# Loading phase and first step of an attention-and-experts kernel, rebuilt: weight halves, subtracts on GpSimd, a second token tile in a buffer of its own

## The reference

```
xn = layernorm(x)
q, k, v = xn@Wq, xn@Wk / sqrt(128), xn@Wv          # 8 heads, DK 128, DV 64
alpha   = sigmoid((xn@Wg + bg) / 16)               # one decay per token and head
state_t = alpha_t * state_(t-1) + k_t v_t^T ; o_t = q_t . state_t
attn    = (o * sigmoid(xn@Wog)) @ Wo
scores  = sigmoid(xn @ gate_w^T) ; sfc = scores + gate_bias
          # keep 4 of 8 groups by the sum of their two best sfc, then the 8 best of 64 experts
ffn     = sum over chosen e (at most 256 tokens each) of weight * (silu(xn@w_gate_e) * (xn@w_up_e)) @ w_down_e
out     = x + attn + ffn
```

## Time and profile before

| | |
|---|---|
| median of 3 runs | 1263.7 us |
| profiled execution, its own time | 1266.82 us |
| span of that execution | 1265.1 us |
| PE busy | 1237.9 us, 98% |
| PEld busy | 1092.2 us, 86% |
| DVE busy | 976.6 us, 77% |
| ACT busy | 624.3 us, 49% |
| POOL busy | 487.4 us, 39% |
| chain that ended last | PE 76%, DVE 16%, issue 5%, ACT 2% |
| DMA | 194.68 MB, mean 154 GB/s |

### The profile page before, as it was taken

One profiled execution on the slowest core, in us unless ns is written; L12 is line 12 of the kernel. 1 busy time (PEld: TensorE's weight loads), 2 busy tenths in 40 slices (PEclk: granted clock), 3 DMA queues, 4 the chain that ended last, 5 costly groups with the idle time before them and its releaser, 6 DMA issues.

```text
span 1265.1 us, 28662 instructions
## 1 busy us (share of the span) xinstructions
PE 1237.9 (98%) x9910; PEld 1092.2 (86%) x9910; DVE 976.6 (77%) x2343; ACT 624.3 (49%) x1319; POOL 487.4 (39%) x377
## 2 busy tenths in 40 slices
PE   7899999999999999999999999999999999999999
PEld 6788888887888888799899998989989999889987
DVE  6997878889797659878688687786885877868844
ACT  6675756666574544344444444444444444434432
POOL 2110111011001027237467385474574754845620
PEclk9999999999999999999999999999999999999999
DMA  6576534354352322357486575674774765748665
GB/s 241 170 250 200 188 110 156 122 190 158 121 171 60 111 75 84 95 145 186 105 198 165 130 178 136 150 181 106 188 171 121 172 155 137 193 104 191 162 194 183
DMA packets 124920, 194.68 MB, mean 154 GB/s; under 512 B 12016, under 2 KB 98608, under 8 KB 124592
## 3 DMA queue, kind: packets, MB, share of 16 engines
q1 hardware_dynamic: 94384, 147.99, 36.1%
q0 software_dynamic: 30464, 45.83, 19.7%
HBM read 148.62 MB, written 57.74 MB: 163 GB/s over the span
## 4 chain that ended last, share of the span: by engine, by line
PE 76%; DVE 16%; issue 5%; ACT 2%; another core or an unknown queue 0%; DVEq 0%; DMA 0%; ACTq 0%
PE bank L793 21%; PE bank L808 7%; PE bank L905 7%; PE bank L937 7%; PE bank L845 6%; PE bank L825 5%; PE bank L877 3%; PE bank L863 3%; PE bank L866 3%; PE bank L948 3%; PE bank L836 3%; DVE Dt L1506 3%; PE bank L889 2%; PE bank L927 2%; DVE At L1527 2%
## 5 line engine op out<-in xcount | busy, mean ns | idle before, releaser
L635 POOL DMA_INDIRECT acc<-arena,idx_all x128 | 224.3, 1752 | 149.4 <-DMA acc<-res 54.1
L627 POOL DMA_INDIRECT arena<-table,idx_all x132 | 163.6, 1240 | 153.8 <-ACT share L1160 96.5
L793 PE MATMUL bank<-xp,wq 128*128 128x512 f32 x768 | 208.4, 406 | 0.0
L793 PE MATMUL bank<-xp,wk 128*128 128x512 f32 x768 | 202.2, 398 | 0.0
L793 PEld LDWEIGHTS bank<-xp,wk 128*128 128x128 f32 x768 | 138.5, 188 | 29.3 <-DVE wk L1416 0.4
L793 PEld LDWEIGHTS bank<-xp,wq 128*128 128x128 f32 x768 | 136.6, 189 | 25.4 <-issue 0.8
L1506 DVE TENSOR_TENSOR_SCAN Dt<-decay,eye_b 128x512 f32<-128x512 f32 x128 | 157.7, 1233 | 0.0
L845 PE MATMUL bank<-qT,kT 128*128 128x128 f32 x1024 | 136.2, 275 | 1.8 <-DVE At L1527 1.4
L1136 ACT ACTIVATE kT<-bank 128x512 f32<-128x512 f32 x128 | 76.7, 599 | 118.0 <-PE bank L793 102.2
L845 PEld LDWEIGHTS bank<-qT,kT 128*128 128x128 f32 x1024 | 125.2, 192 | 3.3 <-DVE At L1527 1.6
L1136 ACT ACTIVATE qT<-bank 128x512 f32<-128x512 f32 x128 | 76.9, 601 | 85.4 <-PE bank L793 64.7
(11 more groups left out here) (174 smaller groups left out, 2317.1 us busy)
## 6 DMA issues: line engine op xcount, KB each, us to landing
decay<-decay_dram SPq DMA_DIRECT2D x64, 512.0 KB
carry<-decay_dram SPq DMA_DIRECT2D x60, 512.0 KB
arena<-in_L_attn_x_dram SPq DMA_DIRECT2D x16, 512.0 KB, 4.5
table<-arena SPq DMA_DIRECT2D x16, 512.0 KB, 3.2
xT_dram<-arena SPq DMA_DIRECT2D x16, 512.0 KB, 3.0
arena<-in_L_ffn_w_gate_dram SPq DMA_DIRECT2D x64, 128.0 KB
arena<-in_L_ffn_w_up_dram SPq DMA_DIRECT2D x64, 128.0 KB
arena<-in_L_ffn_w_down_dram SPq DMA_DIRECT2D x64, 128.0 KB
```

The costliest lines, as they stand in the source:

```text
L627: pool.indirect_dma_start(out=xg[:, e % 2, j, :], out_offset=None, in_=table[:, :], in_offset=bass.IndirectOffsetOnAxis(ap=idx_all[:, e, j ...
L635: pool.indirect_dma_start(out=acc[:, :], out_offset=bass.IndirectOffsetOnAxis(ap=idx_all[:, e, j:j + 1], axis=0), in_=yb[:, e % 2, j, :], ...
L793: last = mm(to[:, :], w[:, part, k, h * DK:(h + 1) * DK], xp[:, other, k, :], start=(k + i == 0), stop=(k == KD - 1 and i == 2))
```

## The change

The loads are issued in another order, with Wv second, and Wq and Wk are loaded and split in two halves of 512 columns (heads 0 to 3 and 4 to 7): q0, k0 first, q1, k1 later. Chunk 1 is loaded at the start into the tile `addend`. The low parts of Wog, q1, k1 and Wo are made by POOL (`weights_low` there, semaphore `w_rest`); the low parts of Wv, q0, k0 stay on DVE. The rounding of q1, k1 and Wo on ACT is moved to `s` = 1, 2, 3 of step 0. The first state is copied by ACT (`state_first`) and not by DVE. On DVE, `route_ranks` and `route_top` of chunk 0 stand ahead of the first scan, and the scans of step 0 have an order of their own (`first_scans`). On PE, the 18 warming transposes become 24, with 6 more ahead of the router, the router no longer waits for ACT's copies, and `decays_across(0)` stands behind the first q projection.

```
-PE_WARM = 18
+PE_WARM = (24, 6)
...
+        raw["q0"] = dt_flat[:, 2 * KD * FEW:3 * KD * FEW].rearrange("p (k n) -> p k n", k=KD)
...
+        raw["q1"] = og_flat[:, 2 * BP:4 * BP].rearrange("p (k n) -> p k n", k=KD)
+        raw["k1"] = res[:, :, :].rearrange("p b d -> p (b d)").rearrange("p (k n) -> p k n", k=KD)
...
+        xt1 = addend[:, :, :]
@@ sync
             sp.dma_start(xt, x_tiles[0]).then_inc(x_loaded, 16)
+            load_weights("v")
             sp.dma_start(gw_rows, gate_w).then_inc(w_const, 16)
-            sp.dma_start(bias_e, ...).then_inc(w_const, 16)
-            sp.dma_start(bias_g, ...).then_inc(w_const, 16)
...
+                if first:
+                    norm_io(1, more=True)
                 load_decay(c, 3)
...
-                    sp.wait_ge(w_split, 5)
+                    sp.wait_ge(w_rest, 4)
...
-            for name, (_, src) in split_of.items():
-                sp.dma_start(raw[name], ...).then_inc(w_in[name], 16)
-            norm_io(0, more=True)
+            for name in ("q0", "k0"):
+                load_weights(name)
+            sp.dma_start(bias_g, ...).then_inc(w_bias, 16)
+            sp.dma_start(bias_e, ...).then_inc(w_bias, 16)
+            sp.dma_start(xt1, x_tiles[1]).then_inc(second_loaded, 16)
+            for name in ("og", "q1", "k1", "o"):
+                load_weights(name)
+            norm_io(0)
@@ gpsimd
+            def weights_low(name):
+                w = split_of[name][0]
+                pool.wait_ge(w_high, list(split_of).index(name) + 1)
+                pool.tensor_tensor(w[:, 1], raw[name], w[:, 0], ALU.subtract).then_inc(w_rest, 1)
...
                     decays_out(STEP_N * c + n)
+                    if is_first(c) and n == 1:
+                        weights_low("o")
...
             decays_out(0)
+            weights_low("og")
+            weights_low("q1")
+            weights_low("k1")
             weights_out(0)
@@ tensor
-            pe.wait_ge(w_const, 64)
+            pe.wait_ge(w_const, 32)
...
             tokens_back(0, 1)
+            for _ in range(PE_WARM[1]):
+                tr(bank[5][:, 0:P], ident[:, :], ident[:, :])
             router(0)
...
+                if is_first(c) and h == H // 2:
+                    pe.wait_ge(w_rest, 2 + which)
...
                 proj_v(c, kind, 0)
                 if first:
-                    decays_across(0)
                     pe.wait_ge(w_split, 2)
                 proj_qk(c, kind, 0, 0)
+                if first:
+                    decays_across(0)
@@ scalar
+            def state_first(p):
+                act.wait_ge(u_ps, p + 1)
+                f(state[:, 2 * p:2 * p + 2], bank[6][:, :].rearrange(...), ACT.Copy).then_inc(state_up, 1)
...
                 if first:
-                    beside(c, kind, 0, 1)
+                    normalise(1)
                     v_copy(c, kind, 3)
-                    normalise(1)
...
+                    if first and s < 4:
+                        weights_high(("q1", "k1", "o")[s - 1])
+                    if first and s % 2 == 0:
+                        state_first(s // 2 - 1)
                     if s % 2 == 0:
                         outs_high(c, s // 2 - 1)
@@ vector
             tokens_kept(1)
+            weights_low("v")
             tokens_low(0)
-            weights_low("v")
-            dve.wait_ge(w_const, 64)
-            weights_low("q")
+            dve.wait_ge(w_bias, 32)
             gates(0)
+            weights_low("q0")
+            weights_low("k0")
             decays_products(0)
-            weights_low("k")
+            statistics(1)
             route_groups(0)
-            statistics(1)
-            weights_low("og")
             scales(1)
+            route_ranks(0)
+            route_top(0)
...
+            def first_scans(s):
+                for c, h in {1: ((0, 2),), 2: ((0, 3),), 3: ((0, 4),), 4: ((0, 5), (0, 6)), 5: ((0, 7), (1, 0)),
+                             7: ((1, 1), (1, 2)), 9: ((1, 3),)}.get(s, ()):
+                    decay_scan(c, h)
...
-            weights_low("o")
-            decay_scan(0, 2)
-            decay_scan(0, 3)
             step(0, "norm")
```

More of the change, by code:

```diff
@@ L254, in build @@
         tab_tiles = table[0:N, :].rearrange("(b c p) w -> c p b w", b=B, c=C)
-        w_in = {name: sem("w_in_" + name) for name in ("v", "q", "k", "og", "o")}
+        w_in = {name: sem("w_in_" + name) for name in split_of}
         w_const, w_ident, consts = sem("w_const"), sem("w_ident"), sem("consts")
+        w_bias, w_rest, second_loaded = sem("w_bias"), sem("w_rest"), sem("second_loaded")
         list_ones, list_consts, sel_zeroed = sem("list_ones"), sem("list_consts"), sem("sel_zeroed")
@@ L448, in step @@
                     load_carry(c, 1)
-                if kind == "norm":
+                if kind == "norm" and not first:
                     norm_io(STEP_N * c + 1, more=True)
@@ L694, in _ @@
             pe.wait_ge(consts, N_CONSTS)
-            for _ in range(PE_WARM):
+            for _ in range(PE_WARM[0]):
                 tr(bank[5][:, 0:P], ident[:, :], ident[:, :])
-            pe.wait_ge(w_const, 64)
+            pe.wait_ge(w_const, 32)
             for k in range(KD):
@@ L720, in router @@
                     pe.wait_ge(gwT_cp, 1)
+                else:
+                    pe.wait_ge(xT_cp, 2 * (c + 1))
                 for b in range(B):
@@ L1070, in normalise @@
                 wait_past(act, xT_ps, 2 * c)
+                source = xt1 if isinstance(c, int) and c == 1 else xt
                 for b in range(B // 2 if is_first(c) else B):
-                    ins = f(xn[:, b, :], xt[:, b, :], ACT.Identity, scale=rstd[:, b:b + 1], bias=shift[:, b:b + 1])
+                    ins = f(xn[:, b, :], source[:, b, :], ACT.Identity, scale=rstd[:, b:b + 1], bias=shift[:, b:b + 1])
                 ins.then_inc(xn_ready, 1)
@@ L1117, in _ @@
             tokens(0, 1)
-            weights_high("q")
+            weights_high("q0")
+            weights_high("k0")
             sigmoids(0)
-            weights_high("k")
+            def state_first(p):
+                act.wait_ge(u_ps, p + 1)
+                f(state[:, 2 * p:2 * p + 2], bank[6][:, :].rearrange("p (b u v) -> p u b v", b=B, u=2), ACT.Copy)\
+                    .then_inc(state_up, 1)
             def select_group(g):
@@ L1232, in step @@
                 if first:
-                    weights_high("o")
+                    beside(c, kind, 0, 1)
                 if kind == "experts":
@@ L1305, in statistics @@
             def statistics(c):
-                dve.wait_ge(x_loaded, 16 * (c + 1))
+                second = isinstance(c, int) and c == 1
+                if second:
+                    dve.wait_ge(second_loaded, 16)
+                else:
+                    dve.wait_ge(x_loaded, 16 if is_first(c) else 16 * c)
                 link, n = chained(norm_chain, c * NORM_CHAIN)
                 for b in range(B):
-                    ins = dve.bn_stats(stats[:, b, :], xt[:, b, :])
+                    ins = dve.bn_stats(stats[:, b, :], (xt1 if second else xt)[:, b, :])
                 link(ins, apart=True)
@@ L1636, in beside @@
                         scales(n)
-                    if (s, place) in ((0, 4), (3, 3), (6, 3)):
+                    if (s, place) in ((0, 4), (3, 3), (6, 3)) and not (is_first(c) and s == 0):
                         route_ranks(n - 1)
@@ L1720, in step @@
                         beside(c, kind, s, 0)
-                    scan_ahead(c, s)
+                    if is_first(c):
+                        first_scans(s)
+                    else:
+                        scan_ahead(c, s)
                     if not early:
@@ L1733, in step @@
                         pair_gated(c, s // 2 - 1)
-                        if not is_last(c):
+                        if not is_first(c) and not is_last(c):
                             pair_state(c, s // 2 - 1)
@@ L1743, in step @@
                         projected(c, s - 4, kind)
+                if is_first(c):
+                    first_scans(H + 1)
             decay_scan(0, 0)
             decay_scan(0, 1)
-            weights_low("o")
-            decay_scan(0, 2)
-            decay_scan(0, 3)
             step(0, "norm")
```

31 lines of the change are left out of this document (16 added, 15 removed).

## The result

| 16 runs each, on the same chip | median | lowest to highest |
|---|---|---|
| before | 1263.78 us | 1261.16 to 1269.72 |
| changed | 1268.09 us | 1263.51 to 1270.50 |

The ratio is 1.0029, 95% interval 1.0019 to 1.0039: slower by 4.3 us by the medians, where 4.7 us less was forecast and the range ended at 1262.5. The profiled execution of the changed kernel took 1264.95 us (span 1263.3), near the lower end of its runs. From step 1 to the end it spends 1171.71 us, against 1177.60 in the profiled execution before, where nothing was changed; the spread of the runs above is as large. So two profiled totals can't be compared here. The start of step 1 was at 87.50 and is now at 91.59, 4.09 us later, which is about the 4.3 of the medians. What follows is read in the first 92 us, with one exception under c1 and c2.

A forecast was written before the change was run, and what follows sets the result against it. PE was taken as the bound from step 1 on (98.7% busy). The update 4.35 us earlier, plus 0.66 idle removed, less 0.3 for ACT, gave 4.7: 1263.7 to 1259.0 us; forecast's range 1257.6 to 1260.6, 8 in 10 1256.5 to 1262.5.

The forecast's parts named there:

- The head: Start up to the first v projection: it starts at 14.05 instead of 15.80 us, after a router of 1.85 us.
- POOL's price: Time of one low-part subtract on POOL: 2.5 us, estimated from its select and cast.
- What it costs DVE: DVE time lost beside POOL's subtracts in step 0: 0.9 us for Wog, 1.0 for each of the other three.
- 6.7 less to do, 3.9 with POOL's toll off: DVE's work before step 1: 6.7 us less, 3.9 after time lost to POOL, and starting 1.7 earlier.
- Up to the update: Step 0 to the first update: second token transpose at 30.95, then 8.4 us of work, update at 39.35 instead of 43.70.
- I count no wait: First scan on DVE, at 27.6: the decays have landed by then, so no wait for their DMA.
- the clock rival: PE's clock does not stay up in step 0, by either of two ways; time 1261, chance 0.16.
- its second way: PE idles 3.0 us before chunk 1's second transpose; some 3.4 us at half speed cost 1.7 us: 1260.7.
- Its first way: PE still at 1.2 GHz in the v and q projections; scan 2.1 us later, 1261.1 us.
- The slower case: POOL's subtracts run at the cast's rate, 4 x 5.5 us, and shut DVE out; 1271 us, chance 0.08.
- nearly whole: From step 1 to the end PE is the bound, so an earlier step 1 reaches the end nearly whole.

The follow-up runs named there:

- c1: b3 without the 24 identity transposes in PE's gap before the tokens of chunk 1; 1261.49 us against 1263.38 before, ratio 0.9977.
- c2: b3 with the loads of q1, k1 and Wo back in the changed kernel's order; 1259.08 us against 1263.38 before, ratio 0.9966.
- a4: The kernel before with only the warming changed: 24 transposes and 6 ahead of the router; 1263.68 us against 1263.23 before, ratio 1.0004.
- a1: The changed kernel with POOL filling the four low parts with zeros instead of subtracting; 1262.0 us against 1263.23 before, ratio 0.9989.
- b4: The changed kernel with POOL copying raw weights into the four low parts instead of subtracting; 1262.13 us against 1264.07 before, ratio 0.9979.
- b3: b2 plus q1, k1, Wo loaded behind the first decay loads, decays_across(0) before the q projection, 24 transposes in PE's first gap; 1258.93 us against 1264.07 before.
- a3: The changed kernel with 24 and 36 identity transposes filling PE's two idle gaps, waits kept; 1265.23 us against 1263.23 before, ratio 1.0017.
- a2: The changed kernel with POOL's four subtracts on DVE, behind the scores of heads 0 to 3; 1263.46 us against 1263.23 before, ratio 1.0010.
- b2: The changed kernel with POOL's subtracts in DVE's idle slots and ACT's rounding of q1, k1 moved; 1261.05 us against 1264.07 before, ratio 0.9977.

## Why the prediction was wrong

**The head held.** The first v projection was put at 14.05 and came at 13.18, in 1.67 us for six (1.6 expected); the decay transpose was put at 16.8 and came at 16.79. The router took 2.00 for 1.85. That the clock would be up by then because PE has no long gap was right: a4, with the same warming but 1.35 us of idle before the router, has v at 14.48 in 2.51 us.

**POOL's price held.** 2.5 us per subtract were expected, 2.37 to 2.42 were measured. The Trainium skill's figure (page "GPSIMD Engine Reference", section "Reconciling with measured numbers"), by which the estimate was 2.25, was nearly as good.

**The step that failed: "What it costs DVE".** The toll was put at 0.9 for Wog and 1.0 for each of the others. It was 1.86 less the operation's own 0.17, 1.7 us; 3.25 - 1.21 = 2.0; about 2.2 for the operation on 32 columns (0.19 by itself); and 3.47 - 2.34 = 1.1 on the last: 7.0 us, against 3.9. Another 1.0 came from POOL's store and cast (0.71 + 0.70 instead of 0.19 each). I had taken a value between nothing and the whole 2.5 from the rows in which POOL *casts*, where the scan grew by 0.37 and no block is seen, and had argued that one input spares DVE. The cast was the wrong model for a subtract: it lets DVE through before it ends (48.30 against 48.91), the subtract doesn't. The statistics with one input were spared (0.38 for four aggregates), but the four-column operation behind them has one input too and was blocked. The Trainium skill, "SBUF — State Buffer", section "Who interferes with whom", says that a two-input DVE instruction and a reading GpSimd one keep each other out for the whole instruction; the traces agree (3.25 and 2.39 us for DVE). For the 1.86, with one input, the same section has another case: a DVE instruction in a 2-port mode, which it says `tensor_scalar` can enter, contends with GpSimd, and the loser waits for the whole instruction. That a1's memset, which reads nothing, holds the same operation until 19.70 agrees with it; no trace shows the mode itself. The prediction quoted the first rule and charged 40% of it.

**What follows from it was missing.** The prediction set the later tolls against DVE's budget, as if DVE's busy time decided when step 1 starts. ("6.7 less to do, 3.9 with POOL's toll off" doesn't add up: 3.0 of toll leaves 3.7, 3.9 leaves 2.8. The sum didn't use it.) The place of the tolls decides: those of q1 and k1, 2.0 + 2.2 us, and the 1.0 of store and cast fall on the stretch from the scan at 39.52 to `gated`. That is why `gated` is late by 5.2 us (49.49, against 44.29 in a1), and ACT and `kT` stand in line behind it. Of the 6.5 us that the changed kernel needs more from the update to step 1 (91.59 - 41.64 = 49.95, forecast 82.8 - 39.35 = 43.45), 4.68 are the idle at 49.7, and 2.6 are the half clock behind it (half of the 5.2 us of work in that window). That is 0.8 more than the 6.5, which I can't place.

**Up to the update.** The first scan came at 28.67 for 27.6: 0.8 of it is the toll, 1.7 on a chain to which I gave 0.9. "I count no wait" held, but narrowly: b4, with less toll, waits 0.19 us for the decays and a1 2.15. The second transpose was 1.15 late. Then the clock rival came by its second way: 3.24 us idle (3.0 worked out), 3.4 us at half. Its first way, v and q at half, did not come. b3 does that stretch in 39.26 - 31.32 = 7.94 us, the changed kernel in 9.54: 1.6 us (1.7 worked out). The forecast had 8.4 for it, so 1.14 were lost there. Together 1.15 + 1.14 = 2.29, and the update is at 41.64 for 39.35.

**The rivals.** The slower case had the right mechanism, POOL shutting DVE out, and the wrong point from which it decides: it was priced by DVE's whole budget and asked for 3.7 us per subtract. It decided at 2.4, because two of the subtracts fall on the chain to `kT`. The clock case was given 0.16 and as an alternative; it came with the toll. No case added the two, and the range didn't reach there.

**By the runs.** From the changed kernel's 91.59: without POOL's subtracts 6.6 less (a1), without the clock's fall 2.9 less (a3), with the subtracts on DVE behind the scores 3.2 less (a2), and with slots, clock, loads and the early decay transpose together 8.8 less (b3). The parts don't add; that a late `kT` hides some of the clock and the reverse is my reading and wasn't tested. That an earlier step 1 is passed on "nearly whole" was too much as well: b3 and c2 lose 1.6 us again in step 6. What stays open is how a1 would run without its 6.8 us of half clock; that wasn't tried. Nor was a subtract on POOL in a stretch in which DVE is idle.

## What to carry to other kernels

Here a subtract on POOL cost VectorE the rest of POOL's 2.4 us from the first instruction that it held, and a four-column operation was enough for that. In such a case price the full time first, charge it to the chain the DVE instruction is on, not to DVE's budget, and then walk the order of the engines that wait behind it. Where a change leaves PE idle for microseconds, count the halved clock behind it as well, and compare a filled gap with an empty one: 24 transposes without use moved step 1 by 4.5 us here, and the median by some 2.4. If a change shifts an early stretch of a long kernel, compare where that stretch ends, since the profiled totals differ by more than the change, and then check against the medians whether the gain arrives at the end.

## What the runs showed of the hardware

- The granted clock fell to half after each PE idle of 3.24 us and more between 24 and 60 us (3.24, 3.25, 3.41, 4.09, 4.42, 4.68, 4.79, 5.11). The length of one idle doesn't decide alone: the clock fell after 1.79 us in b3 and 1.78 in c2, and not after 1.78 at the same place in b2 and c1; it fell in a4 after 1.35 and 0.48 us with the router between, and not after the 1.43 of the earlier trace rows. The half-speed stretch lasted about 3.4, 6.8 or 10.2 us, and not longer for the longer gap: 3.4 after 3.24, 10.2 after 4.42, 6.8 after 5.11.
- With 24 transposes of the identity in the gap (2.78 us in b3 and c2) the granted clock stayed at 1.00 from 24 to 60 us in a3, b3 and c2.
- A write alone on POOL (a1's memset, 0.95 us) left the scan beside it at its 1.22 us; a copy (1.04 us) made it 1.87; the two-input subtract (2.40 us) made it 3.25. The four-column operation with one input took 0.17 us by itself, 0.38 beside the memset and 1.86 beside the subtract.
- Beside a subtract on POOL, the statistics' aggregates (0.38 us for four) and the multiplication with an operand in PSUM (0.69) kept their length.
